# A GRU recurrence on one core: gate inputs as rows from DRAM seeded a step ahead, the candidate in two parts

## What is computed

```
gi = x @ W_ih + b_ih                 # no dependence on h
gh = h @ W_hh + b_hh
r = sigmoid(i_r + h_r);  z = sigmoid(i_z + h_z)
n = tanh(i_n + r * h_n)
h = (1 - z) * n + z * h              # 512 times, one after the other
```

## Time and profile before

| | us |
|---|---|
| median of 3 runs (3906.92 to 3917.58) | 3907.85 |
| the profiled execution | 3908.48 |
| its span in the trace | 3906.8 |
| gate inputs stage | 0 to 100.06 |
| GRU: set-up, then the steps | 100.06 to 1901.60 |
| everything after | 1901.60 to 3906.80 |

### The profile page before, as it was taken

The page is one execution under the profiler, slowest core; times in us unless marked ns, Lnnn a source line. Parts: engine busy times, 40 slices in busy tenths (PEclk is TensorE's granted clock), DMA queues, the critical chain, the costliest instruction groups (busy, mean ns, idle before and its releaser), DMA issues. The chain is left out here.

```text
span 3906.8 us, 168625 instructions
## 1 busy us (share of the span) xinstructions
PE 3668.3 (94%) x69056; PEld 2363.5 (60%) x69087; DVE 2267.9 (58%) x5855; ACT 1507.9 (39%) x5283; POOL 506.0 (13%) x1077
## 2 busy tenths in 40 slices
PE   7899999999999999999799999968899999889999
PEld 3788888888888888887534444324433333455554
DVE  2566666666666666666477777745366666542228
ACT  0344444444444444444344444532344444321110
POOL 0011111011111110110022222210000000024430
PEclk9999999999999999999899999989999998999999
DMA  4700000000000000001111111102111111159987
GB/s 115 258 0 0 0 0 0 0 0 0 0 0 0 0 0 0 0 0 32 56 39 38 56 38 42 33 10 91 49 50 55 48 55 58 50 172 306 316 249 291
DMA packets 130517, 244.83 MB, mean 63 GB/s; under 512 B 18613, under 2 KB 72129, under 8 KB 126483
## 3 DMA queue, kind: packets, MB, share of 16 engines
q1 hardware_dynamic: 109874, 190.92, 14.5%
q10 hardware_dynamic: 9760, 25.70, 2.3%
q0 software_dynamic: 10816, 27.33, 2.2%
HBM read 147.92 MB, written 50.33 MB: 51 GB/s over the span
## 5 line engine op out<-in xcount | busy, mean ns | idle before, releaser
L311 PE MATMUL gru_prz<-ahead,h 128*4 128x160 f32 x16384 | 747.4, 300 | 9.8 <-DVE h L429 9.8
L311 PE MATMUL gru_pn<-ahead,h 128*32 128x128 f32 x16384 | 635.5, 273 | 0.0
L311 PEld LDWEIGHTS gru_pn<-ahead,h 128*32 128x32 f32 x16384 | 490.0, 110 | 34.7
L311 PEld LDWEIGHTS gru_prz<-ahead,h 128*4 128x4 f32 x16384 | 387.2, 87 | 147.3 <-DVE h L429 20.6
L410 DVE STREAM_TRANSPOSE gru_tr<-gru_prz 128x160 f32<-128x160 f32 x512 | 179.1, 350 | 467.4 <-PE gru_prz L311 467.4
L311 PE MATMUL gru_pz<-ahead,h 128*4 128x96 f32 x16384 | 432.7, 246 | 6.6 <-issue 6.6
L366 ACT ACTIVATE gru_rn<-gru_pre 128x16 f32<-128x16 f32 x512 | 119.7, 234 | 745.6 <-DVE gru_pre L413 745.6
L311 PEld LDWEIGHTS gru_pz<-ahead,h 128*4 128x4 f32 x16384 | 363.1, 87 | 8.5 <-issue 7.3
L943 DVE TENSOR_REDUCE da_mx<-da_ps 128x2 f32<-128x1024 f32 (+3 forms) x256 | 201.3, 817 | 131.8 <-PE da_ps L636 131.8
L272 POOL COPY gru_pick<-ident 128x4 f32 x512 | 96.5, 188 | 1374.1 <-PE gru_pz L304 1368.2
L429 DVE TENSOR_TENSOR_SCAN h<-gru_d 128x16 f32<-128x16 f32 (+1 forms) x1024 | 236.2, 231 | 51.6 <-ACT gru_d L373 0.7
(11 more groups left out here) (314 smaller groups left out, 5699.6 us busy)
## 6 DMA issues: line engine op xcount, KB each, us to landing
ahead<-in_L_ffn_gate_up_proj SPq DMA_DIRECT2D x64, 768.0 KB, 8.1
yk<-gru_zeros SPq DMA_DIRECT2D x6, 4096.0 KB, 31.6
ex_wd<-in_L_ffn_down_proj ACTq DMA_DIRECT2D x64, 384.0 KB, 7.5
ahead<-yk SPq DMA_DIRECT2D x16, 1536.0 KB, 8.7
ahead<-wide SPq DMA_DIRECT2D x15, 1024.0 KB, 4.7
ahead<-xnT SPq DMA_DIRECT2D x15, 1024.0 KB, 4.5
da_wg<-ahead SPq DMA_DIRECT2D x45, 256.0 KB, 4.8
fa_wg<-ahead SPq DMA_DIRECT2D x45, 256.0 KB, 4.7
```

Source lines behind the costliest of these rows:

```text
L311: last = nc.tensor.matmul(rows(j), of(c), whh[:, c, j, cols], start=False, stop=True, skip_group_check=True)
```

## The change

**The step.** `prz` now has two buffers, used by alternate steps, and holds r and all of z. A buffer is filled before its step with the r and z inputs, biases included, by one ACT copy of 256 columns from `rows`; `pn` has two buffers too, filled with the n bias in the same way. So the z products (300, 304), the add of the r input on DVE (413), and the ACT copies of inputs (360, 361) are gone; one sigmoid of 20 columns takes r and the first z together. POOL copies the n input of each step. DVE transposes and scans n in two parts, group 0 (32 and 16 columns) and groups 1 to 3 (96 and 48), and tanh has two parts as well; h's first part waits for the first tanh alone.

**The next block's inputs.** The weights and tokens of `next_gate_input` come from fixed buffers: SP copies a 256 KB column block of W_ih within SBUF every fourth step (`fill_weights`), POOL the tokens twice a block. The r inputs are now made as rows, gathered in `r_stage`, stored to DRAM in `gi_rows` and loaded from there to `rows` with z's. `yk` is zeroed in 24 pieces of 1 MB in blocks 1 to 3, one behind each `fill_weights`.

**The gate inputs stage.** Four chunks (n) instead of eight; then 17 rounds of rows (one of r, 16 of z), each written by DVE to one of three staging buffers (`NS`) and stored to `gi_rows` by SP. On SP these stores stand behind the 64 transfers of W_hh and 16 small ones of the bias rows.

```
+            sp.wait_ge(zero_set, 2)
+            for j in range(KD):
+                for b in range(B):
+                    sp.dma_start(t.bias_rows[32 * j + 8 * b + 6:32 * j + 8 * b + 7, :],
+                                 b_hh[2 * D + j * P:2 * D + (j + 1) * P].unsqueeze(0)).then_inc(bh_in, 16)
+            for q in range(NQ):
+                sp.wait_ge(row_out, q + 1)
...
+                sp.dma_start(t.rows_dram[kb].rearrange("b t j f -> (b t) j f")[:, :, gate * P:(gate + 1) * P],
+                             stage[:, q % NS, :].rearrange("p (j f) -> p j f", j=KD)).then_inc(stored[q % NS], 16)
+                if q == 2:
...
+                    for j in range(KD):
+                        sp.dma_start(t.rows[32 * j:32 * j + B, 0:32, :], t.rows_dram[0][:, :, j, :]).then_inc(first_in, 16)
...
-            for kb in range(T // 32):
-                if kb >= 2:
-                    pe.wait_ge(z_out, kb - 1)
+            for q in range(NQ):
+                kb, cols = (0, slice(0, D)) if q == 0 else (q - 1, slice(2 * D, 3 * D))
+                if q >= 2:
+                    pe.wait_ge(row_out, q - 1)
...
+            for q in range(NQ):
+                dve.wait_ge(row_psum, q + 1)
+                if q >= NS:
+                    dve.wait_ge(stored[q % NS], 16 * (q // NS))
+                nc.vector.tensor_tensor(stage[:, q % NS, :], pg[:, 2 + q % 2, :], t.gi_rbias[:] if q == 0 else rowb[:, 0, D:2 * D],
+                                        ALU.add).then_inc(row_out, 1)
...
+            def fill_weights(kb, c):
+                if kb * NG + c > 0:
+                    sp.wait_ge(gi_psum, kb * NG + c)
+                to = right if c < KD else left
+                sp.dma_start(to[:], wih[:, :, c * P:(c + 1) * P]).then_inc(weights_in, 16)
...
             def step(s, par):
...
                 pe.wait_ge(h_ready[0], s * 1 + 1)
+                pe.wait_ge(rz_seeded, s * 1 + 1)
+                pe.wait_ge(n_seeded, s * 1 + 1)
                 part(rz_rows, after, RZ, (0,))
-                pe.wait_ge(seeded, s * 1 + 1)
...
             def next_gate_input(kb, c, k):
                 if k == 0:
+                    pe.wait_ge(weights_in, kb * (16 * NG) + c * 16 + 16)
+                    pe.wait_ge(tokens_in, ((kb * NG + c) >> 2) + 1)
                     pe.wait_ge(gi_out, kb * NG + c + 1)
-                    pe.wait_ge(wst_ready, kb * NG + c + 1)
...
+            def step(s, par):
...
+                nc.scalar.activation(prz[:, 1 - par, R0:Z2], t.rows[:, bass.ds((s + 1) & 63, 1), :].rearrange("p o f -> p (o f)"),
+                                     ACT.Copy).then_inc(rz_seeded, 1)
...
+                nc.scalar.activation(cb(rd[:, 0:ST + B, 2]), tr[:, :, 0:B], ACT.Sigmoid).then_inc(rz_act, 1)
+                for n, part in enumerate(PARTS):
+                    of = slice(part.start * B, part.stop * B)
+                    act.wait_ge(narg_done[n], s * 1 + 1)
+                    nc.scalar.activation(d0[:, of, 2:4], narg[:, of, 3:4].broadcast_to([P, of.stop - of.start, 2]), ACT.Tanh).then_inc(tanh_done[n], 1)
```

More of the change, by code:

```diff
@@ L126, in _ @@
             pe.wait_ge(xT_ready, B * KD)
-            for c in range(NG):
+            for c in range(KD):
                 if c >= 2:
@@ L142, in _ @@
         @block.scalar
         def _(act):
[L144 to L150, removed]
@@ L274, in _ @@
[L274 to L285 removed]
+            pool.wait_ge(set_up, 5)
@@ L287, in _ @@
+            with pool.Fori(0, NBL - 1) as kb:
+                for half in range(2):
+                    fill_tokens(kb, half)
+                    with pool.Fori(0, 16) as n:
+                        gate_input_of_n(kb * 32 + n + half * 16)
+            pool.wait_ge(gi_out, (NBL - 1) * NG + 1)
+            with pool.Fori(T - 32, T) as s:
+                gate_input_of_n(s)
         @block.tensor
         def _(pe):
-            pe.wait_ge(loaded, 16)
-            pe.wait_ge(tn_done, 1)
-            for j in range(KD):
-                last = nc.tensor.matmul(pn[32 * j:32 * j + 32, 0:P], one[:], bias[:, j, :], start=True, stop=True)
@@ L379, in _ @@
+                act.wait_ge(tz_done, s * 1 + 1)
+                nc.scalar.activation(cb(d1[:, B:ST, 2]), tz[:, :, 0:B], ACT.Sigmoid).then_inc(z_act, 1)
+            with act.Fori(0, T // 2) as q:
+                for par in range(2):
+                    step(q * 2 + par, par)
         @block.vector
         def _(dve):
-            nc.vector.memset(bias[:], 0.0).then_inc(bias_set, 1)
-            nc.vector.memset(one[:], 0.0).then_inc(bias_set, 1)
-            dve.wait_ge(bias_set, 2)
-            nc.vector.memset(one[0:1, 6:8 * B:8], 1.0).then_inc(bias_set, 1)
@@ L414, in step @@
                 dve.wait_ge(n_rows, s * 1 + 1)
-                nc.vector.transpose(tn[:], pn[:, 0:P]).then_inc(tn_done, 1)
-                dve.wait_ge(tn_done, s * 1 + 2)
-                dve.wait_ge(r_act, s * 1 + 1)
-                dve.wait_ge(gin_ready, s * 1 + 1)
-                nc.vector.tensor_tensor_scan(narg[:].rearrange("p c o -> p (c o)"), tn[:, 0:KD * 32:2],
-                                             rn[:].rearrange("p c o -> p (c o)"), 0.0, ALU.mult, ALU.add).then_inc(narg_done, 1)
+                for n, part in enumerate(PARTS):
+                    cols = slice(part.start * 32, part.stop * 32)
+                    nc.vector.transpose(tn[:, cols], pn[:, par, cols]).then_inc(tn_done[n], 1)
@@ new lines, in step @@
+                for n, part in enumerate(PARTS):
+                    of = slice(part.start * B, part.stop * B)
+                    dve.wait_ge(tn_done[n], s * 1 + 2)
+                    if n == 0:
+                        dve.wait_ge(rz_act, s * 1 + 1)
+                        dve.wait_ge(gin_ready, s * 1 + 1)
+                    nc.vector.tensor_tensor_scan(narg[:, of, :].rearrange("p c o -> p (c o)"), tn[:, part.start * 32:part.stop * 32:2],
+                                                 rn[:, of, :].rearrange("p c o -> p (c o)"), 0.0, ALU.mult, ALU.add).then_inc(narg_done[n], 1)
```

277 lines of the change are left out of this document (137 added, 140 removed).

## The result

The changed kernel took 4011.41 us (median of 4 runs, 4008.55 to 4014.53), the kernel before 3908.85 beside it: 1.0257 times as long, 95% interval 1.0244 to 1.027. The forecast was 3838 us, with a range of 3805 to 3905. The change made the kernel 2.6% slower.

A forecast was written before the change was run, and what follows sets the result against it. The prediction took the loop from h through PE's products and n's chain back to h as the bound; 3908.5 - 97.5 (steps) - 1 (set-up) + 28 (row stage) = 3838 us, range 3805 to 3905.

The forecast's parts named there:

- What bounds the step: Main loop: h to PE's products, n's chain and back to h sets the 3.40 us; PE's other work fits its wait.
- The step: Main loop: splitting n starts h at +0.86 instead of +0.94 behind `tn`; step from 3.40 to 3.28 us, bounds 3.25 to 3.40.
- The overlap of two DVE instructions: DVE: the second instruction of a pair starts about 0.07 us before the first ends, where no operand is missing.
- Rival D: DVE between `tn` and h: instructions run one by one, step 3.68 to 3.70 us, total 4047 us; chance 0.10.
- The rule on operation count: DVE: the skill's "Minimize op *count*", since the "DRAIN happens regardless"; by it, splitting n costs.
- Loop ends and the rest: Steps stretch: of 55 us beyond the plain steps, 10 (loop ends, 0.08 for each of 120) and 9 (all else) stay.
- The row stage: Gate inputs stage: stores wait behind W_hh and small transfers, PE stands; end at 126 to 128.5 instead of 100, +28 us.
- I take 2.6: hidden, at no cost: Weights by DMA: SP's 256 KB copy every fourth step lands in 2.6 us, with 0.3 us to spare.
- Rival C: Weights by DMA: landing at 4.8 us, PE waits 1.9 us 120 times, +228, total 4066 us; chance 0.10.
- The chances: Whole kernel: faster 0.75, same (3896 to 3920 us) 0.08, slower 0.17.

The follow-up runs named there:

- whole n: Changed kernel with only the split of n undone (one transpose, one scan, one tanh, h's first part waiting for it): 4058.85 us.
- the strided loads: Changed kernel with a block's four row loads cut by batch row, each to partitions 32 apart instead of 4 neighbouring ones: 3860.92 us.

## Why the prediction was wrong, step by step

**What bounds the step** was read rightly. h is the releaser in the long run, removing PE's and ACT's work alone changes nothing (whole n: 3.40), and a shorter path to h does.

**The step**: forecast 3.28, measured 3.28 to 3.29, by both of its terms: h at +0.86, and PE's product 0.21 behind h's start instead of 0.25. The overlap of two DVE instructions, read from a single pair, carries over: two transposes of 0.217 and 0.240 us in the mean take 0.38 together. Rival D is out; the split is nearly free here. The rule on operation count, quoted in the prediction from the Trainium skill (VectorE: DVE Perf Modes, "Rules for kernel authors"), did not decide.

**Loop ends and the rest**: I let 19 us stand. A step behind a loop end takes 3.42 us, 0.14 more than the others instead of 0.08, which is 7 us more over 120, and the entry into the last loop costs another 5. With these 12 us and the 10 us of the row stage (next) on top of 3838 the changed kernel would have been at 3860, and with the strided loads, which end the waits in the blocks, it was at 3860.92. That the two agree this closely is in part luck: what follows the steps takes from 2003 to 2012 us in the profiles, in code that is the same.

**The row stage**: forecast +28, measured +38.3. The forecast mechanism is there in its place (PE idle from 57 to 78), and with the four loads off SP's queue the stage ends at 126.47. That this lies in the forecast 126 to 128.5 is in part luck: the 16 small transfers took 4.82 us instead of 7.2, so the first buffer came free at 77 instead of 80, and PE's rounds and the end of the stage took that much longer. The other 12 us are the loads, which my own list of SP's order contains, between the third store and the fourth. I priced the stores and passed over them.

**The step that failed** is "I take 2.6: hidden, at no cost". The 2.6 us is right to the digit for a fill on its own. But I set its slack against the fill alone, and never asked what else SP issues between two fills. The eight rounds of a block are not alike: in one, four loads of 128 KB go out ahead of the next fill, take 18.7 us where the round has 13.3, and the fill lands 10.7 us after its issue. In the whole working, `load_rows` has no price. It cost 123.7 us of PE's waiting, and 150 us with the steps at the lower clock (4011 against 3861 with the loads cut the other way). Rival C had the right wait and the right sign, but from another cause, and so another size: a fill late by its own length 120 times, instead of 15 times by what stood ahead of it.

No row of before would have given the loads' rate: none there writes 128 KB to 4 partitions. The estimate of 27 GB/s at the strided loads above needs no run, though, and gives 19 us for the four. Without it, what could have been known is that they are four transfers on the queue of a wait with 0.3 us to spare, and that the rows leave their price open. A bound from the rows would have run from 2.1 us each (256 KB alone), which hides, to 4.8 each, 19 for the four, which does not. The forecast range should have held both.

**The chances**: 0.75 for faster rested on a sum with one term left out, which no weighing of the other terms could mend.

## What to carry to other kernels

When a transfer is put on a queue with little slack, write down the queue's whole order for one period, round by round, and give every entry a duration; a small slack belongs to the worst round, not the usual one. Count what other queues have under way at that time as well: moving slow loads to another queue took them out of the order, but stores beside them still landed late. Look at the shape of a transfer as well as its bytes: how many partitions it reaches, and whether they lie apart. And where one instruction's wait sets the loop, work taken off the other engines is worth only what it lets start earlier.

## What the runs showed of the hardware

- 128 KB to 4 neighbouring partitions moves at 28 GB/s, to 4 partitions 32 apart at 55 GB/s, both with about a quarter of the DMA engines; the same pieces spread over 128 partitions land in 2.5 us.
- A 256 KB store that lands in 2.6 us with nothing beside it took 15.9 to 18.8 us behind loads to 4 neighbouring partitions on its own queue, and 8.1 to 14.4 us with these loads on POOL's queue.
- A PE that waited 8 us came back at a granted clock of 0.52, and the step behind took 5.10 us in the mean instead of 3.28; 15 such waits cost 150 us instead of 124.
- With 12 transfers issued 3.3 us ahead of PE's entry into the last loop step 481 took 7.5 us, with them held back 3.28; but two kernels had such transfers there without a long step.
